# Two adaLN layers on one core: layer 1's first norms moved into layer 0's FFN, roots on VectorE, and a reordered opening

## The reference

```
mod = silu(c) @ wmod                 -> sa, ca, ga, sb, cb, gb (256 each)
ga, gb = sign(g) * max(|g|, 0.25)
x = x + ga * attention(layernorm(x) * (1 + ca) + sa)
x = x + gb * ffn(layernorm(x) * (1 + cb) + sb)
layer 0: attention  16 heads, 4 key/value heads of 128, rotary, causal, scale 128**-0.5
         ffn        h = silu(x @ Wg) * (x @ Wu); of each 4 neighbours the 2 largest stay; h @ Wd (1024 wide)
layer 1: attention  h = norm_scale * x / (rms(x) + 1e-8) * split_scale; 4 heads, 2 key/value heads of 64,
                    no mask; x + out @ Wo.T
         ffn        a shared expert and 7 routed ones, top 2, capacity 1024 / 7
```

## Time and profile before

| | |
|---|---|
| median of 3 runs | 777.65 us |
| the profiled execution | 778.5 us, of which the span is 776.7 |
| mean granted clock of TensorE | 0.992 |
| stages in the profiled span | opening 0 to 34, attention 0 to 444.2, FFN 0 444.5 to 532.0, norm block 532.3 to 551.7, attention 1 552.1 to 693.5, FFN 1 693.9 to the end |

### The profile page before, as it was taken

How to read it: one execution, slowest core, us unless ns; L and a number is a source line. 1 busy time by engine, 2 the same in 40 slices (tenths; PEclk the granted TensorE clock), 3 DMA queues, 4 the chain that set the end, 5 groups by cost and what they waited for, 6 DMA issues and landing times. The chain is left out here.

```text
span 776.7 us, 12379 instructions
## 1 busy us (share of the span) xinstructions
PE 721.5 (93%) x4376; PEld 620.7 (80%) x4376; DVE 556.8 (72%) x1263; ACT 447.5 (58%) x924; POOL 372.5 (48%) x403
## 2 busy tenths in 40 slices
PE   6979989999999999999999799999979999789997
PEld 4858878888888888888888689997768778577787
DVE  4656786678766787767776788776579788566666
ACT  2756656667566676666655343322578776546432
POOL 2685556635766357653451330002756545205773
PEclk8999999999999999999999999999999999999999
DMA  7000000000000000004000040004100000000001
GB/s 250 14 8 8 8 22 15 14 2 14 22 15 8 8 15 14 14 8 170 7 8 8 9 128 1 1 1 126 39 0 2 1 1 1 0 4 0 1 1 55
DMA packets 19115, 19.85 MB, mean 26 GB/s; under 512 B 2158, under 2 KB 17006, under 8 KB 19054
## 3 DMA queue, kind: packets, MB, share of 16 engines
q1 hardware_dynamic: 17934, 18.40, 7.3%
q10 hardware_dynamic: 1120, 0.66, 0.3%
HBM read 18.01 MB, written 1.05 MB: 25 GB/s over the span
## 5 line engine op out<-in xcount | busy, mean ns | idle before, releaser
L633 ACT ACTIVATE at_probs<-at_probs,at_negmax 128x128 f32<-128x128 f32 (+7 forms) x128 | 99.6, 778 | 31.8 <-DVE at_negmax L736 29.7
L935 POOL TENSOR_TENSOR at_swapped<-at_swapped,at_sin 128x512 f32<-128x512 f32 x40 | 52.1, 1302 | 136.0 <-ACT at_swapped L611 136.0
L736 DVE CUSTOM_DVE_ANT_0 at_probs<-at_scores,causal 128x128 f32<-128x128 f32 (+7 forms) x128 | 96.1, 751 | 16.8 <-PE at_scores L59 16.2
L524 PE MATMUL at_turn<-ident_sb,at_probs 128*128 128x128 f32 x576 | 85.0, 274 | 13.2 <-DVE at_full_T_lo L752 11.1
L524 PEld LDWEIGHTS at_turn<-ident_sb,at_probs 128*128 128x128 f32 x576 | 66.5, 140 | 21.8 <-issue 8.4
L626 ACT ACTIVATE at_edge_T_hi<-at_turn 128x128 fp32r<-128x128 f32 (+3 forms) x128 | 55.5, 434 | 33.2 <-PE at_turn L524 32.8
L57 PE MATMUL at_scores<-at_kT_hi,room 128*128 128x512 f32 (+1 forms) x192 | 66.4, 346 | 3.4 <-DVE at_negmax L736 3.4
L626 ACT ACTIVATE at_full_T_hi<-at_turn 128x512 fp32r<-128x512 f32 x64 | 38.3, 598 | 49.5 <-PE at_turn L524 47.4
L58 PE MATMUL at_scores<-at_kT_lo,room 128*128 128x512 f32 (+1 forms) x192 | 66.7, 347 | 0.0
L59 PE MATMUL at_scores<-at_kT_hi,room 128*128 128x512 f32 (+1 forms) x192 | 66.3, 345 | 0.0
L752 DVE TENSOR_TENSOR at_edge_T_lo<-at_turn,at_edge_T_hi 128x128 fp32r<-128x128 f32 (+3 forms) x128 | 61.3, 479 | 1.1 <-ACT at_edge_T_hi L626 0.8
(11 more groups left out here) (405 smaller groups left out, 2292.3 us busy)
## 6 DMA issues: line engine op xcount, KB each, us to landing
at_wq_in<-L_attn_Wqkv SPq DMA_DIRECT2D x16, 128.0 KB, 2.2
at_wo_in<-L_attn_Wo SPq DMA_DIRECT2D x16, 128.0 KB, 2.0
staging<-L_ffn_routed_w SPq DMA_DIRECT2D x7, 256.0 KB, 4.8
ff_wmod<-L_wmod SPq DMA_DIRECT2D x1, 1536.0 KB, 6.2
at_wmod<-L_wmod SPq DMA_DIRECT2D x1, 1024.0 KB, 8.6
staging<-L_ffn_w_gate SPq DMA_DIRECT2D x1, 1024.0 KB, 5.2
staging<-L_ffn_w_up SPq DMA_DIRECT2D x1, 1024.0 KB, 7.3
staging<-L_ffn_w_down SPq DMA_DIRECT2D x1, 1024.0 KB, 9.7
```

Of the source, the lines that this page charges most:

```text
L524: mm = pe.transpose(p_turn[t % 2][:, b - b0, :], probs[:, s % 4, b * P:(b + 1) * P], m.ident[:, :])
L633: act.activation(row, row, ACT.Exp, scale=-1.0, bias=negmax[:, unit % 4:unit % 4 + 1], accum_out=rowsum[:, unit // NT % 2, i:i + 1])\
L736: dve.tensor_tensor_reduce(out=probs[:, s % 4, 0:width], in0=p_scores[s % 2][:, 0:width], in1=m.causal[:, S - width:], scale=-1.0, scalar= ...
L935: turning = pool.tensor_tensor(swapped[:, r % 2, :], swapped[:, r % 2, :], sin[:, cols], ALU.mult)
```

## The change

*Roots.* All square roots of variances leave ScalarE. `inverse_roots` starts from an integer operation on the bits of variance + epsilon, and takes three Newton steps: eleven small instructions in a chain on VectorE.

*Opening.* x comes in two loads: tiles 0 to 3 on SP, tiles 4 to 7 on ScalarE's queue behind both c; identity and mask follow there, ahead of the silu. The exp table is loaded right after the silu. TensorE issues three warm products, the first modulation columns, two warm products, and then turns x. On VectorE no statistics of tiles 4 to 7 stand ahead of the first norms any more; the aggregation and root of these tiles follow the low halves of the first rows, and then the cosine product comes ahead of wv's low half.

*Layer 1's modulation.* Its row columns of wmod (1 MB, sa, ca, ga, gb) are loaded at the end of attention 0, into the room of the key buffers. GpSimd makes the wide silu(c) there. TensorE's row products stand in `ffn0`'s head in place of most of its warm products, around the turning of x, in the two banks of the down products; ScalarE reads them after the first silu. The columns follow the last up product.

*Norms of layer 1 inside `ffn0`.* A `Late` object holds what both stages share. Rows 0 to 511 (tiles 0 to 3) are normed, modulated, scaled, turned and split within `ffn0`: VectorE `row_roots(0)` and `row_roots(1)`, ScalarE `normalize`, `mean_squares`, `roots`, `turned_hi`, GpSimd `mod_rows`, the scaling of g, the low halves; TensorE `turn_g` in unit 7. Tiles 4 and 5 get as far as h. The small weights, the split of the attention weights, the bounds of both gates and the scaling and splitting of wo are done in `ffn0` too, mostly on GpSimd.

*`attention1`.* The norm block with its warm products is gone, and the meeting of the engines behind it. Its one block starts with the adds of the last two tiles, their norms, and four jobs of the first half of the rows (`early_jobs`), then `turn_g` for the second half. Six jobs stand ahead of the slots now. *`ffn1`* loads no sigmoid table; attention 1 does, at its end.

```diff
-def inverse_roots(dve, m, chain, tiles, n):
+def inverse_roots(dve, m, chain, tiles):
...
+    chain.run(dve.tensor_scalar(vareps, var, EPS, None, ALU.add))
+    chain.run(dve.tensor_scalar(rstd.bitcast(as_int), vareps.bitcast(as_int), -0.5, float(0x5F3759DF), ALU.mult, ALU.add))
+    for _ in range(3):
+        chain.run(dve.scalar_tensor_tensor(out=rough, in0=rstd, scalar=-0.5, in1=vareps, op0=ALU.mult, op1=ALU.mult))
+        chain.run(dve.tensor_tensor(rough, rough, rstd, ALU.mult))
+        chain.run(dve.scalar_tensor_tensor(out=rstd, in0=rough, scalar=1.5, in1=rstd, op0=ALU.add, op1=ALU.mult))
# attention0, SyncE
-                for half in range(2):
-                    sp.dma_start(m.x[:, 4 * half:4 * half + 2, :], x_rows[:, 4 * half:4 * half + 2, :]).then_inc(x_in[half], 16)
+                sp.dma_start(m.x[:, 0:4, :], x_rows[:, 0:4, :]).then_inc(x_in[0], 16)
...
+                            sp.dma_start(row_wmod[:, :, 0:3 * DM], late_rows[:, :, 0:3 * DM]).then_inc(m.mod_in, 16)
+                            sp.dma_start(row_wmod[:, :, 3 * DM:], late_rows[:, :, 5 * DM:]).then_inc(m.mod_in, 16)
# attention0, TensorE
-                keep_warm(pe, early_banks[1], m.causal, 5)
+                keep_warm(pe, early_banks[1], m.causal, 3)
                 pe.wait_ge(wmod_in[0], 16)
                 pe.wait_ge(c_silu, 1)
                 mod_columns(0)
+                keep_warm(pe, early_banks[1], m.causal, 2)
                 pe.wait_ge(const_in, 32)
# attention0, VectorE
+                inverse_roots(dve, m, chain, FIRST_TILES)
                 for n in FIRST_TILES:
                     dve.tensor_scalar(xn[:, n, :], m.x[:, n, :], m.meanvar[:, n, 0:1], m.rstd[:, n:n + 1],
                                       ALU.subtract, ALU.mult).then_inc(normed, 1)
                 columns(1)
...
+                inverse_roots(dve, m, chain, LAST_TILES)
                 spread(dve, m, LAST_TILES).then_inc(rstd_done, 1)
+                dve.wait_ge(tables_in[0], 32)
+                cos_rope(0, 0, early_banks[0], proj_free)
                 dve.wait_ge(wv_hi, 1)
                 dve.tensor_tensor(wv.lo, wv_in[:, :, :], as_f32(wv.hi), ALU.subtract).then_inc(wv_ready, 1)
# ffn0, TensorE
-                keep_warm(pe, idle_bank, m.room, 7)
+                pe.wait_ge(m.mod_in, 32)
+                mod_rows(0)
                 turn_x(0)
                 turn_x(1)
-                keep_warm(pe, idle_bank, m.room, 9)
+                mod_rows(1)
+                keep_warm(pe, p_gate[:, 0:2, :].rearrange("p e t -> p (e t)"), m.room, 2)
...
+                    if u == 7:
+                        turn_g()
# ffn0, VectorE
+                def row_roots(c):
+                    tiles = (2 * c, 2 * c + 1)
+                    stats(c)
+                    variances(dve, m, chain, tiles)
+                    inverse_roots(dve, m, chain, tiles)
+                    spread(dve, m, tiles).then_inc(rstd_done, 1)
...
                     multiply(u)
+                    if u in (3, 5):
                         add(c - 1)
+                    if u == 5:
+                        row_roots(1)
+                    if u == 6:
+                        inverses()
+                    if u == 7:
+                        stats(2)
+                        variances(dve, m, chain, (4, 5))
                     sparsify(u)
+                    if u == 1:
+                        small_weights()
+                    if u == 3:
+                        row_roots(0)
+                    if u == 6:
+                        add(2)
+                inverse_roots(dve, m, chain, (4, 5))
# ffn0, GpSimd, behind the scaling of w_down
+                pool.wait_ge(mod_read, 3)
+                bounded_gate(0)
+                pool.wait_ge(w_hi, 2)
+                pool.tensor_tensor(late.wq.lo, late.wq_in, as_f32(late.wq.hi), ALU.subtract)
+                pool.tensor_tensor(late.wv.lo, late.wv_in, as_f32(late.wv.hi), ALU.subtract)
+                low_x(2)
...
+                chain.run(pool.tensor_scalar(late.wo.hi, late.wo_in, 1.0, 1.0, ALU.mult, ALU.mult))
+                mod_rows(0)
+                pool.wait_ge(up_mm, 6)
+                chain.step(pool.tensor_tensor(late.wo.lo, late.wo_in, as_f32(late.wo.hi), ALU.subtract))
+                mod_rows(1)
+                pool.wait_ge(late.inverted, 1)
+                for n in FIRST_TILES:
+                    pool.tensor_scalar(g_row[:, n, :], late.h_row[:, n, :], late.inv[:, n:n + 1], 1.0, ALU.mult, ALU.mult).then_inc(g_done, 1)
# attention1, TensorE
+                for n, job in enumerate(early_jobs):
+                    project(n, *job)
+                turn_g()
+                for n, job in jobs_of(-1)[len(early_jobs):]:
                     project(n, *job)
```

More of the change, by code:

```diff
@@ L139, in build @@
         m = Shared(x, ident, causal, modcol, gate, stats, meanvar, vareps, rstd, tiny, hT,
[L140 removed]
+                   staging, staging1, staged, staged1, gate_w, expert_bias, gate_in, mod_row, tables, w2_gated, room, chain, nbias, csil, ones, staging_at, pool_chain, cwide, mod_in)
         attention0(nc, a, m, sems, sb, split)
[L142 to L143 removed]
+        with ExitStack() as two:
+            late = Late(nc, m, sems, sb, split, two)
+            ffn0(nc, a, m, late, sems, sb, split)
+            attention1(nc, a, m, late, sems, sb, split)
         ffn1(nc, a, m, sems, sb, split)
@@ L254, in attention0 @@
         wq, wk, wo = pair("wq", [P, KD, P]), pair("wk", [P, KD, P]), pair("wo", [P, DM])
-        kT = [pair(f"kT{n}", [P, S]) for n in range(2)]
         q = [Split(m.room[:, 2 * n * S:(2 * n + 1) * S], m.room[:, (2 * n + 1) * S:(2 * n + 2) * S]) for n in range(2)]
@@ L263, in attention0 @@
         att = pair("att", [P, 2, S])
+        kT_at = nc.sbuf_base
+        kT = [pair(f"kT{n}", [P, S]) for n in range(2)]
+        row_wmod = m.row_wmod = nc.alloc_sbuf_tensor_at("row_wmod", [P, KD, 4 * DM], F32, offset=kT_at)
         values = nc.alloc_sbuf_tensor_at("at0_v", [P, KV0, 2, NT, D0], F32R, offset=m.staging_at)
@@ new lines, in mean_squares, with roots @@
+                def mean_squares(c):
+                    for n in (2 * c, 2 * c + 1):
+                        act.wait_ge(h_done, 2 * n + 2)
+                        act.activation(g_row[:, n, :], late.h_row[:, n, :], ACT.Square, accum_out=late.squares[:, n:n + 1]).then_inc(late.squared, 1)
+                def roots():
+                    act.wait_ge(late.squared, 4)
+                    act.activation(late.root[:, 0:4], late.squares[:, 0:4], ACT.Sqrt, scale=1.0 / DM).then_inc(late.rooted, 1)
@@ L1172, in _, with turned_hi @@
+                def turned_hi():
+                    act.wait_ge(col_done, 1)
+                    for k in range(KD):
+                        act.wait_ge(g_mm, k + 1)
+                        act.activation(g32[:, k, :], p_g[k], ACT.Copy, scale=late.norm_col[:, 2, k:k + 1]).then_inc(g32_done, 1)
+                        act.wait_ge(g32_done, k + 1)
+                        act.activation(m.hT.hi[:, k, 0:BANK], g32[:, k, :], ACT.Copy).then_inc(g_hi, 1)
                 act.wait_ge(m.staged, 32)
@@ L1615, in attended_hi, with mean_squares, roots, normed_rows @@
                     act.activation(att.hi[:, chunk // 2 % 2, chunk % 2 * BANK:(chunk % 2 + 1) * BANK], p_att[:, :], ACT.Copy).then_inc(att_hi, 1)
+                def mean_squares(tiles):
+                    for n in tiles:
+                        if n >= 6:
+                            act.wait_ge(h_done, n - 5)
+                        act.activation(g_row[:, n - 4, :], h_row[:, n, :], ACT.Square, accum_out=late.squares[:, n:n + 1]).then_inc(late.squared, 1)
+                def roots():
+                    act.wait_ge(late.squared, 8)
+                    act.activation(late.root[:, 4:NT], late.squares[:, 4:NT], ACT.Sqrt, scale=1.0 / DM).then_inc(late.rooted, 1)
+                def normed_rows():
+                    act.wait_ge(late.inverted, 2)
+                    for n in (6, 7):
+                        act.activation(g_row[:, n - 4, :], h_row[:, n, :], ACT.Copy, scale=late.inv[:, n:n + 1]).then_inc(g_done_act, 1)
+                def turned_hi():
+                    for k in range(KD):
+                        act.wait_ge(g_mm, k + 1)
+                        act.activation(gT.hi[:, k, BANK:S], p_g[k], ACT.Copy, scale=late.norm_col[:, 2, k:k + 1]).then_inc(g_hi, 1)
+                job_high(0, *jobs[0])
+                mean_squares((4, 5))
+                job_high(1, *jobs[1])
+                mean_squares((6, 7))
+                roots()
+                job_high(2, *jobs[2])
+                normed_rows()
+                job_high(3, *jobs[3])
+                turned_hi()
                 load_table(act, m, ACT.Exp, 1)
-                for n, job in jobs_of(-1):
+                for n, job in jobs_of(-1)[len(early_jobs):]:
                     job_high(n, *job)
```

509 lines of the change are left out of this document (240 added, 269 removed).

## The result

The changed kernel takes 782.96 us (median of 5 runs, 781.43 to 784.06) against 777.65 before (5 runs, 776.88 to 779.37): 1.0066 times as long, 95% interval 1.0048 to 1.0083. So it is 5.3 us slower where 2.5 us faster was forecast. The profiled execution took 784.06 us, its span is 781.9 (before: 778.5 and 776.7).

The account below looks back on a forecast made before the run. TensorE was taken to pace the FFN, VectorE its head, with VectorE becoming the FFN's bound after the change. Terms -2.6 + 12.6 - 12.4 + 0.8 - 2.5 + 1.6 = -2.5 gave 775.2 us; 8-in-10 range 767 to 785.

Parts of the forecast that it names:

- Opening, -2.6: Kernel start: earlier mask and roots on VectorE bring the first value product from 25.00 to about 22; bounds 4.1 and 0.
- First multiply, +5.5: Layer 0's FFN head: first half's root +1.05, second half's root beside GpSimd +4.0, last instruction lengthened +0.5; multiply at 464.2.
- Units 0 to 2, +2.6 for the clock: Layer 0's FFN after the first multiply: TensorE idles some 6 us, then half clock for a while costs 1.7 to 3.4.
- rival B: Layer 0's FFN: VectorE and GpSimd serialize, 13.5 instead of 7.2 and 2.0 more in units 0 to 2; 783.5, chance 0.20.
- Rest of the FFN: Last five units of layer 0's FFN: VectorE becomes the bound, 47.9 plus 7.2 waiting for GpSimd; block ends at 544.9.
- Norms and first jobs, -12.4: Attention 1's start: block start to first maximum of the scores takes 17.2 instead of 29.6 us; bounds 10.5 and 13.5.
- the clock +0.8: Attention 1's start: TensorE's clock may be low after idling while VectorE finishes the FFN; 0 to 1.5 us.
- Slots, -2.5: Attention 1's first slots: no 1.25 us wait for GpSimd's wo split, one key job fewer, 1.25; bounds 1 and 3.
- Tails, +1.6: Two more bare roots: end of attention 1 +0.5, start of the last FFN +1.1.
- Rival A: Layer 0's FFN stays bound by TensorE, new work falls into VectorE's slack; block ends at 538.6, 768.9 us, chance 0.22.
- Rival C: Opening gives nothing: clock is low before the turning and its half speed eats the earlier rows; 777.8, chance 0.14.
- the marks set for the result: Signs expected in the trace: turning before 13 us, value product 22 to 23, roots 0.6 to 0.7, block 12 to 13 later.

Follow-up runs that it names:

- experiment 4: Changed kernel plus warm products (results unread) in TensorE's idle stretches, fewer behind attention 1's last turning: 778.45 us, ratio 1.0007 to the kernel before.
- experiment 2: Changed kernel with GpSimd's FFN work cut (no gate bounds or wo scaling, one-column rows; output differs): 773.12 us, ratio 0.9932 to the kernel before.
- experiment 6: Changed kernel with GpSimd's scaling and splitting of wo and bounds of gate gb moved from layer 0's FFN into attention 1: 777.32 us, ratio 0.9997.
- experiment 5: Changed kernel with the last two roots (end of attention 1, start of last FFN) back on ScalarE's square root: 778.81 us, ratio 1.0009.
- experiment 1: Changed kernel with GpSimd scaling w_down at the end of attention 0 instead of in the FFN's head: 779.04 us, ratio 1.0016.

## Why the prediction was wrong

The forecast named the right mechanism (VectorE becomes the FFN's bound, GpSimd's company is its largest cost), and the sign was wrong: 7.7 us between -2.5 and +5.2 of span. By its own steps:

- *Opening, -2.6.* -1.1 measured at attention 0's end. Up to the first value product the sum came out (21.9 worked out, 21.88 measured), partly by luck: the turning came 0.7 us later than the sum had it, and in eight other traces with this opening and no filler there the value product stands at 21.6 to 22.5. The step that failed is its silence on the clock behind that product, where a slow stretch at 22 to 26 us costs 1.6. 1.5 us of the miss.
- *First multiply, +5.5.* 3.4 measured from attention 0's end. The first half's root is 1.0 longer, as forecast. The second was priced at 4.5 and took 2.4 more: GpSimd's products were over after eight of the eleven instructions, and from the start of the norms to the multiply 2.03 us pass instead of 2.53. 2.1 us too much in the sum. That the first multiply stands near its mark (460.98, marked 464.2 less 2.6) is two errors that meet.
- *Units 0 to 2, +2.6 for the clock.* 4.3 measured, and none of it the clock: with the clock held (experiment 4) these units took 27.7 us, without 27.3. It is VectorE beside GpSimd's new work, for which the sum had no term here (only rival B had one, 2.0). The scaling of wo costs 1.6 of it: without it (experiments 2 and 6) the units took 25.7. The rest is read from the rows alone, beside the splits of wq, wv and wk. 1.7 us of the miss.
- *Rest of the FFN, 55.1 us from the fourth multiply to the block's end.* 56.9 measured. Both terms were a little small: VectorE's own work 47.9, and 48.9 in experiment 2; GpSimd's company 7.2, and 8.0 by that experiment. (Part of the 48.9 is what GpSimd keeps there.) 1.8 us of the miss. (The lower bound of 538.6 for no waiting does not follow from the terms, which give 489.8 + 47.9 = 537.7.)
- *Norms and first jobs, -12.4, the clock +0.8.* -10.0 in place of -11.6. VectorE's chain came out as worked out (turning of g 9.2 us behind the block's start, forecast 9.7). The failed term is the clock: twelve job products at 0.43 us each cost 2.5 us, not 0.8. 1.6 us of the miss.
- *Slots, -2.5.* -1.9 measured, from the first maximum to the last add. 0.6 us of the miss; no run takes it apart.
- *Tails, +1.6.* 3.9 measured; experiment 5 shows all of it to be the two roots. Of these, 1.7 us are TensorE's turning and filler at half clock, behind a wait of 2.48 us that was 1.38 before. The prediction had put a price on the roots and none on what they do to TensorE. 2.3 us of the miss, the largest single one; the last 0.3 lie in the last FFN's end.

So two steps failed. The first is the clock. It was priced in the FFN's head, at 2.6, where it cost nothing since VectorE was as late, and at 0.8 in attention 1's head. Where TensorE was the engine waited for, it cost 1.6, 2.5 and 1.7 us: 5.8 in place of 3.4. The second is GpSimd's company in the FFN: units 0 to 2 had no term for it. They lost 4.3 us, and the 2.6 booked there for the clock and the 2.1 too much for the root hid that from the sum.

Rival B came out at 783.5, beside the measured time, but not by its mechanism: it wanted the FFN 8.3 us later than the forecast, and it was 1.4; its 2.0 more in units 0 to 2 is the part that was true. Rival A's block end (48.8 us behind the fourth multiply) is what experiment 2 gives once the company is gone (48.9), though VectorE is then still busy for 45.0 of the 47.5 us to the last down product, so TensorE does not bound it; the conclusion fell because GpSimd's work met the sums and not the multiplies. Rival C is true of the sum in the changed kernel, and false of the opening itself. Of the marks set for the result, the turning of x (12.93), the value product (21.88), the root's instructions (0.67) and the block's end (12.8 later) were met; the 17 us to the first maximum were 19.6.

What stays open: why a given wait of 2.1 us is followed by a slow stretch in one schedule and not in another. The runs show that it repeated in two traces of the same kernel and was elsewhere in another schedule, no more.

## What to carry to other kernels

A gain made by moving work into another stage's slack has to be charged twice: for each GpSimd instruction that now meets VectorE, up to its whole duration on VectorE's path (0.67 for 0.16, 2.62 for 0.41), and for each bare wait that TensorE gets, the products behind it at half speed if TensorE is waited for there, and nothing where it isn't. Look first for a place where the other engine is idle (17.2 us ahead of the scaling of w_down, 29.7 us ahead of its first work in attention 1), then shorten the chain itself (one Newton step fewer in each of eight roots was worth 7.8 us, at the price of a less exact root), and only then fill with warm products: those were worth 4.5 us alone and nothing once the rest was done.

## What the runs showed of the hardware that was not expected

The stretch at half clock does not follow from the wait just ahead of it alone. After waits of 2.12 and 0.96 to 1.13 us the job products ran at 0.50 in the changed kernel (twice) and in the kernels of experiments 1, 2, 5 and 6, whose schedules stand up to 11 us apart; after the same waits with the old opening they ran at 1.00. That one kernel differs in two ways that the runs don't separate: its schedule stands 2.0 us later there than the changed one's (1.4 at attention 0's end), and its clock had already fallen 12 us earlier, behind a wait of 2.63 us after which it stayed up in the changed kernel. Either way the 1.4 us that the opening lost were won back 100 us later, and a difference of 1 to 2 us between two schedules says little of the part that was changed, until the clock of both is compared stretch by stretch.
